# The last residual of the closing steps added on VectorE, not by identity matmuls

## What is computed

```python
out = relu(bn1(conv1x1(x, w1)))                 # 1024 -> 256
offset = conv3x3(out, w_off) + b_off            # 256 -> 18
out = deform_conv3x3(out, offset, w2)           # 4 bilinear corners x 9 taps, 256 -> 256
out = relu(bn2(out))
y = relu(bn3(conv1x1(out, w3)) + x)             # 256 -> 1024
```

```python
out = relu(gconv1x1(y * m1, gw1))               # 1024 -> 256
out = relu(gconv3x3(out * m2, gw2)) * m2        # 256 -> 256
result = relu(gconv1x1(out, gw3) + y)           # 256 -> 1024, the last residual
```

## Time and profile before

| | |
|---|---|
| median of 3 runs | 3089.85 us (3082.94 to 3093.89) |
| profiled execution | 3089.26 us, span 3087.4 us |
| granted TensorE clock, mean | 0.973 |
| TensorE busy | 2848.4 us, 92% |
| VectorE busy | 2312.3 us, 75% |
| ScalarE busy | 1294.4 us, 42% |
| GpSimd busy | 1240.7 us, 40% |
| moved by the transfers | 907.19 MB, mean 294 GB/s |
| identity matmuls of the last residual (L573) | 160 instructions, first at 2450.0 us |

### The profile page before, as it was taken

How to read it: one execution, slowest core, us unless ns; L and a number is a source line. 1 busy time by engine, 2 the same in 40 slices (tenths; PEclk the granted TensorE clock), 3 DMA queues, 4 the chain that set the end, 5 groups by cost and what they waited for, 6 DMA issues and landing times.

```text
span 3087.4 us, 45424 instructions
## 1 busy us (share of the span) xinstructions
PE 2848.4 (92%) x12064; PEld 1568.1 (51%) x12064; DVE 2312.3 (75%) x5439; ACT 1294.4 (42%) x2530; POOL 1240.7 (40%) x1160
## 2 busy tenths in 40 slices
PE   6876999999999999999999999999998999999998
PEld 3334555555555555555555555555555555555553
DVE  2116888888887878888777878877888888888871
ACT  1113444444444444444444444444444444444442
POOL 1005443433443434344344344434444455555540
PEclk9988999999999999999999999999999999999999
DMA  8889888888898888889888888888887788888872
GB/s 295 252 257 339 315 307 302 295 311 306 284 327 303 304 300 304 309 283 324 301 293 297 312 295 303 320 299 297 308 322 271 277 302 294 306 288 300 298 269 82
DMA packets 297888, 907.19 MB, mean 294 GB/s; under 512 B 33795, under 2 KB 107651, under 8 KB 289027
## 3 DMA queue, kind: packets, MB, share of 16 engines
q0 software_dynamic: 165888, 604.05, 55.7%
q1 hardware_dynamic: 113408, 234.35, 22.5%
q10 hardware_dynamic: 18432, 67.12, 5.4%
HBM read 747.72 MB, written 157.68 MB: 293 GB/s over the span
## 4 chain that ended last, share of the span: by engine, by line
PE 60%; DMA 15%; DVE 9%; issue 7%; POOL 3%; ACT 2%; SPq 2%; DVEq 0%; ACTq 0%; POOLq 0%
DMA corners<-corner_tables,samples_in 13%; PE psR L518 9%; PE psD L498 7%; PE psD L500 7%; PE psD L499 7%; PE psA L410 6%; PE psR L550 6%; PE psV L479 6%; DVE val L949 5%; PE psA L446 4%; PE psR L531 4%; PE psR L567 3%; POOL corners L375 3%; DMA y<-in_x 2%; SPq L340 2%
## 5 line engine op out<-in xcount | busy, mean ns | idle before, releaser
L375 POOL DMA_INDIRECT corners<-corner_tables,samples_in x1152 | 1228.7, 1067 | 1750.1 <-DVE val L949 1257.6
L949 DVE SCALAR_TENSOR_TENSOR val<-corners,samples_in,val 128x256 f32<-128x256 f32 x3456 | 1429.2, 478 | 239.5 <-ACT val L695 204.4
L695 ACT ACTIVATE val<-corners,samples_in 128x256 f32<-128x256 f32 x1152 | 522.1, 505 | 396.2 <-DMA corners<-corner_tables,samples_in 390.0
L709 ACT ACTIVATE valT_hi<-psV 128x512 fp32r<-128x512 f32 x576 | 311.5, 592 | 775.1 <-PE psD L500 623.7
L518 PE MATMUL psR<-deformed,w_sb 128*128 128x512 f32 x1024 | 491.2, 622 | 60.2 <-DVE y L880 51.0
L959 DVE TENSOR_TENSOR valT_lo<-psV,valT_hi 128x512 fp32r<-128x512 f32 x576 | 370.1, 684 | 203.0 <-ACT valT_hi L709 201.3
L498 PE MATMUL psD<-valT_hi,w_hi 128*128 128x512 f32 x1152 | 487.8, 423 | 0.4 <-DVE valT_lo L959 0.4
L499 PE MATMUL psD<-valT_hi,w_lo 128*128 128x512 f32 x1152 | 458.9, 398 | 0.0
L500 PE MATMUL psD<-valT_lo,w_hi 128*128 128x512 f32 x1152 | 458.6, 398 | 0.0
L479 PEld LDWEIGHTS psV<-const_sb,val 128*128 128x128 f32 x2304 | 266.2, 143 | 237.0 <-issue 131.4
L479 PE MATMUL psV<-const_sb,val 128*128 128x128 f32 x2304 | 313.4, 279 | 69.9 <-DVE valT_lo L959 64.9
(11 more groups left out here) (78 smaller groups left out, 1540.9 us busy)
## 6 DMA issues: line engine op xcount, KB each, us to landing
corner_tables<-x_sb SPq DMA_DIRECT2D x256, 256.0 KB
y<-in_x SPq DMA_DIRECT2D x128, 512.0 KB, 7.7
out<-y ACTq DMA_DIRECT2D x128, 512.0 KB, 5.2
x_sb<-in_x SPq DMA_DIRECT2D x48, 1024.0 KB
corners<-corner_tables,samples_in POOLq DMA_INDIRECT x1152, 5.9
corner_tables<-corners SPq DMA_DIRECT2D x8, 2244.5 KB, 14.1
y<-in_x SPq DMA_DIRECT2D x8, 2048.0 KB, 11.0
samples_dram<-samples SPq DMA_DIRECT2D x32, 90.0 KB, 7.9
```

Source lines behind the costliest of these rows:

```text
L375: nc.gpsimd.indirect_dma_start(corners[:, slot, :], None, table, bass.IndirectOffsetOnAxis(ap=index[:, TAPS * t + k:TAPS * t + k + 1], axi ...
L695: nc.scalar.activation(val[:, (bpar + k) % 2, tile, :], corners[:, n % GS, 0:CMID], ACT.Copy, scale=samples_in[:, bpar, w:w + 1]).then_inc ...
L709: nc.scalar.activation(valT_hi[:, m, :], psV[m][:], ACT.Copy).then_inc(valT_ready, 1)
L949: nc.vector.scalar_tensor_tensor(acc, corners[:, n % GS, corner * CMID:(corner + 1) * CMID], samples_in[:, bpar, w:w + 1], acc, ALU.mult, ...
```

## The change

In the closing steps the identity matmuls are gone, gconv3 closes its sum, and out_add runs on VectorE, as in the steps with A. All waits that distinguished the two forms now wait for out_sum, the count of additions. ScalarE's order of output ReLUs in the closing steps becomes that of the steps with A: all eight at the end of the step. In VectorE's beside[8] the additions are put in between.

```diff
@@ conv3, on TensorE
-                        pe.wait_ge(out_sum if "A" in on else out_ready, KC * e - 1 + m)
+                        pe.wait_ge(out_sum, KC * e - 1 + m)
@@ gconv2
-                            pe.wait_ge(out_ready, KC * e)
+                            pe.wait_ge(out_sum, KC * e)
@@ gconv3
-                        pe.wait_ge(out_sum if "A" in on else out_ready, KC * e + 2 * i)
+                        pe.wait_ge(out_sum, KC * e + 2 * i)
                     for half in range(2):
                         rows = slice(64 * half, 64 * half + 64)
-                        mm = pe.matmul(psR[half][:], gw3_sb[rows, bank, chunk], gb[rows, bank, :],
-                                       start=True, stop="A" in on)
-                        if "A" in on:
-                            mm.then_inc(g3_done, 1)
-                    if "A" not in on:
-                        for half in range(2):
-                            pe.matmul(psR[half][:], ident, y[:, par, 2 * i + half, :], start=False, stop=True
-                                      ).then_inc(g3_done, 1)
+                        pe.matmul(psR[half][:], gw3_sb[rows, bank, chunk], gb[rows, bank, :],
+                                  start=True, stop=True).then_inc(g3_done, 1)
@@ out_relu, on ScalarE
-                    act.wait_ge(out_sum if "A" in on else g3_done, KC * e + m + 1)
-                    total = y[:, par, m, :] if "A" in on else psR[m % 2][:]
-                    nc.scalar.activation(y[:, par, m, :], total, ACT.Relu).then_inc(out_ready, 1)
+                    act.wait_ge(out_sum, KC * e + m + 1)
+                    nc.scalar.activation(y[:, par, m, :], y[:, par, m, :], ACT.Relu).then_inc(out_ready, 1)
@@ ScalarE's order, steps without A
-                    before = {7: each(out_relu, 0, 1), 8: each(out_relu, 2, 3)}
+                    before = {}
                     after = {
...
-                        8: each(out_relu, 4, 5),
                     }
-                    last = each(deformed_relu, 0, 1) + each(out_relu, 6, 7)
+                last = each(out_relu, 0, 1, 2, 3, 4) + each(deformed_relu, 0, 1) + each(out_relu, 5, 6, 7)
@@ out_add, on VectorE
-                    if "E" not in on or "A" not in on:
+                    if "E" not in on:
                         return
@@ VectorE's order, steps without A
-                    beside[8] += c1[8] + c2[8] + each(valT_low, 8) + c3[8] + [coordinates]
+                    beside[8] += each(out_add, 0, 1) + c1[8] + each(out_add, 2, 3) + c2[8] + each(
+                        valT_low, 8) + c3[8] + each(out_add, 4, 5, 6, 7) + [coordinates]
```

More of the change, by code:

```diff
@@ L755, in step @@
                     after = {}
-                    last = each(out_relu, 0, 1, 2, 3, 4) + each(deformed_relu, 0, 1) + each(out_relu, 5, 6, 7)
                 else:
-                    before = {7: each(out_relu, 0, 1), 8: each(out_relu, 2, 3)}
+                    before = {}
                     after = {
```

## The result

The changed kernel takes 3143.51 us (median of 4 runs, 3141.57 to 3151.05), 1.0168 times the time before [1.0149, 1.0187]. It is slower, as forecast, but by 1.7% and not 0.6%: above the upper end of the range, 3132 us. The profiled execution took 3143.94 us, its span is 3142.1 us, 54.7 us more than before; the mean granted clock fell from 0.973 to 0.954.

A forecast was written before the change was run, and what follows sets the result against it. Bound: in steps 32 to 39 the gather loop through VectorE, GpSimd and ScalarE; in 40 and 41 the order TensorE, VectorE, ScalarE. 3089.26 us plus 7 x 4.5 + 0.5 - 13.7 = +18.3 gives 3107.6 us, range 3076 to 3132.

The forecast's parts named there:

- The sum: Whole forecast: seven boundaries at +4.5 us, boundary 39/40 +0.5 us, end -13.7 us, together +18.3 us; chance 0.48.
- The load behind the late store: Closing-step boundaries: store 0 goes out late, the residual's load lands late, y_add(0) starts 6.2 us later.
- The slack of 1.7 us: Tap after y_add(0): VectorE's waits of 0.55 and 1.16 us take up 1.7 us of the delay, leaving 4.5.
- I count nothing, up to 0.5 us: Tail, valT_copy(8): turn_val(8) and tap(7) some 1.5 us late, ScalarE late anyway; priced at nothing, up to 0.5 us in range.
- VectorE as the bound: Rival, seven boundaries: all eight additions are paid on VectorE, 38.5 us, giving 3114.6 us; chance 0.17.
- Its mark: Sign in the tail for the VectorE rival: c3[8] is 1 us or more late each time.
- Load in time: Rival, seven boundaries: store and load together stay below 7.1 us, nothing stays, 3076 us; chance 0.17.
- half: Rival, seven boundaries: store and load take 9 us or lighter traffic helps; 1.5 us stay each, 3086.6 us; chance 0.18.
- the worst transfers: Upper bound per boundary: store and load take 13.2 to 14 us, gathers land no earlier; 9.5 us stay.
- Boundary 39/40: Between steps 39 and 40, without gathers: late store and load against earlier conv3(0), +0.5 us, between -1 and +2.
- The end: Steps 40 and 41: pairs take 1.93 and not 3.73 us; with the last pair, 13.7 us saved.
- the last pair's 1.1: Last pair of the end: 2.6 us to the last store where it takes 3.7 today, 1.1 us saved.

The follow-up runs named there:

- e2: Changed kernel with the residual of chunks 0 to 3 loaded into the free buffer x_sb in the closing steps: ratio 1.0040 to the kernel before.
- e9: Changed kernel with the first residual loads into x_sb, first additions one place earlier and first four output ReLUs ahead of corner0(10): ratio 0.9999 to the kernel before.
- e11: Changed kernel with out_add(0,1) moved into tap 7 and out_add(2,3) to the head of tap 8, nothing else: ratio 1.0109 to the kernel before.
- e5: Changed kernel with first additions and first four output ReLUs both earlier, load still into y: ratio 1.0029 to the kernel before.
- e3: Changed kernel with a pair of unread matmuls ahead of gconv3(1) to (3) and conv3(0) from step 33: ratio 1.0158 to the kernel before.
- e10: e9 with one unread matmul behind each gconv3 pair in steps 40 and 41: 3082.09 us, ratio 0.9968 to the kernel before.
- e4: Kernel before without the identity matmuls of the closing steps and nothing in their place, last residual missing: ratio 0.9973 to the kernel before.
- e7: e2 with the unread matmul pairs of e3 ahead of gconv3(1) to (3) and conv3(0): ratio 1.0104 to the kernel before.

## Why the forecast was right in sign and wrong in size

The sum had a boundary as 6.2 us by which y_add(0) comes later, less 1.7 us of slack behind it: 4.5 us. Measured over the six boundaries from step 33 on, as means:

| stretch, us | before | changed | difference | forecast |
|---|---|---|---|---|
| valT_low(7) to y_add(0) of the next step | 18.50 | 26.95 | +8.45 | +6.2 |
| y_add(0) to valT_low(7) | 59.41 | 60.01 | +0.60 | -1.7 |

Both terms failed, by 2.3 us each.

**The load behind the late store: the mechanism is right, its size was not.** y_add(0) is released by the load in each of the seven steps, and e2 takes 5.0 us per boundary away by moving the first two loads. That 5.0 is near 4.5 is luck, since the parts of the sum were off. In the tail worked through, the last gathered tile reaches ScalarE 11.4 us after valT_low(7) (11.2 forecast) and the store goes out at 13.1 us (12.9 forecast). But the store landed in 3.7 us (5.0 taken), the load in 9.5 (6.4 taken), together 13.2 against 11.4, at the upper end of the earlier trace rows. The load was taken as half quiet since GpSimd would issue no gathers beside it; GpSimd did pause for 11.4 us, but the later stores and loads ran beside it.

The single-DMA fit of the Trainium skill (DMA: Bandwidth & Descriptors, "Anatomy of one DMA") would have left nothing. That section gives the fit for transfers issued from GpSimd, and these are issued by ScalarE and SyncE; 13.2 us where the estimate from it is 6.4 speak against using it for transfers beside gathers and stores.

**The slack of 1.7 us: this step failed.** It was to stay saved, and it is saved for one tap only. y_add(0) to y_add(2) is 7.6 us, before 9.4. But VectorE's waits for gathered tiles only move: per step 1.7 us of them stood between y_add(0) and valT_low(1) and 0.2 us between valT_low(1) and valT_low(2); now it is none and 1.5 us. A tap that starts early stands waiting at the next gathers, which aren't issued before VectorE has freed their slots, late as it was in the tail; this reason is argued from the loop, the moved wait is measured. The sum had looked at one tap of the loop and not at the next.

**"I count nothing, up to 0.5 us": this step failed.** It saw that gconv3(1) would wait for out_add(0,1) and that turn_val(8) and tap(7) stand behind it, 1.5 us late, which is what the trace shows. It then took the delay as covered by ScalarE's idle time, and put no price on the clock behind the wait: tap(7) ends 3.1 us late and ScalarE covers 1.2. c3[8] was to stay within 0.5 us; it is 2.0 us late. out_add(0,1) was put where VectorE had waited 2.08 us, which is free for VectorE, but TensorE needs it 3.67 us earlier than it gets it. In the changed kernel this lies under the wait for the load. Without that load, in e2, it comes to light, together with the ReLUs ahead of `deformed`, for which conv3(0) waits 2.31 us, and makes 4.1 us per boundary. e9 shows it: with additions and ReLUs both early, and the load aside as in e2, the boundary falls from 82.0 to 77.84.

| boundary, us | ReLUs late | ReLUs early |
|---|---|---|
| additions late | 86.3 to 87.0 | 81.7 |
| additions early | 84.0 | 80.2 |
| additions late, load aside | 82.0 | |
| additions early, load aside | | 77.8 |

The costs overlap and don't add, and so the terms of the sum can't be priced one by one: early additions give 2.3 to 3.0 us with late ReLUs and 1.5 with early ones. With late ReLUs the wait for the load grows and takes the rest (58.3 us in e11), with early ones the wait for `deformed` behind the late gather (5.04 us in e5). How the 4.1 us divide between TensorE's wait and the ReLUs before `deformed` is open; no run has the load aside and only one of the two early.

**VectorE as the bound.** Its mark, c3[8] over 1 us late, is in the trace, its mechanism isn't: in e3 fillers alone bring c3[8] back to within 0.7 us of its place before, and e9 runs all eight additions at no cost. The mark couldn't tell VectorE's load from TensorE's wait for VectorE. *Load in time* and *half* are out: 3.7 us for the first store, and 38.9 us of waits. The range was too narrow by a slip as well: its upper end of 3132 us was said to be 6.4 us per boundary, but 6.4 us give 3121 us by the sum's own terms, and 3132 us are 8.0. The measured 8.7 lie beyond either, below the 9.5 us that the bounds had for the worst transfers.

**Boundary 39/40:** +1.1, within the -1 to +2 given.

**The end: -13.7 became -3.8.** The term has two errors. The pair was worked out at 1.93 us, as if the first addition followed a first half of gconv3 at 0.57 us. There is no such half: the matmuls for the two banks, 64 partitions each, run side by side. Two instructions start together at 3103.47 (window 3103.40 to 3103.60), the other two 0.53 us later, and both banks are complete at 3104.6. The addition follows at 3104.63:

```profile
3103.47 0.70 PE L567 MATMUL psR<-gb,gw_sb 64*128 64x512 f32 x2 [1.37 <-DVE gb L915]
```

```profile
3104.63 1.29 DVE L923 TENSOR_TENSOR y<-psR,y 128x512 f32<-128x512 f32 x2 [1.22 <-PE psR L567]
```

1.16 us to the first addition and 1.34 to the next gconv3 make 2.50. With 3.73 - 2.50 = 1.23 us per pair, 7 pairs would still give 8.6 us, and 9.7 with the last pair's 1.1. The rest went to the clock, which the sum left out: at 0.73 gconv3 takes 2.08 us and gconv2 9.32. With the clock at 1.00, in e10, the end gives 42.4 - 33.4 = 9.0 us, which nearly closes the account of 9.7. The Trainium skill has this rule in TensorE: Matmul & The Clock Gate, "Part 1: The HAM clock gate": two levels, and a busy TensorE is what brings the higher one; trace and runs agree, with 0.73 in the changed kernel's end and 1.00 in e10's. So the identity matmuls had been doing two jobs, and taking them away gave back less than their busy time (e4).

## What to carry to other kernels

When work moves to a later place, follow its result to the last transfer that waits for it: here a ReLU's store, by it the next load into the same buffer, by it the first operation of the next step; a load into a free buffer breaks that chain. A slot that is idle on the engine that takes the work isn't free if the engine that needs the result waits there: read the place from the consumer's queue. Slack that is found in one tap of a loop is only saved if the next tap doesn't wait for the same loop. And before TensorE work is removed from a chain of short hand-overs, count the clock as part of its price; one unread matmul that ends before the wait does gave it back at the end of this kernel, while fillers in a queue that was needed (e7) gave back the clock and no time.

## What the runs showed of the hardware

- One unread float32 matmul in each 1.4 us gap raised the granted clock of the end from 0.73 (last 39 us of e9) to 1.00 (last 34 us of e10), and took gconv2 of step 41 from 10.77 to 7.96 us, with the pairs no further apart.
- Behind a wait of 3.67 us the granted clock was 0.72 over 6 us, and turn_val(8) with tap(7) took 5.5 us where they took 3.8 at 1.00.
- A 512 KB load beside landing gathers, three stores and a second load landed in 9.5 us, 2.5 times the 3.8 us of a quiet one.
- Two float32 matmuls of 64 partitions each, on different halves of the partitions and into different banks, start together and are both done 1.13 us later, and the addition that reads the first bank starts at 1.16 us.
